# A graph layer on one core: the masks of four tiles by one compare, the degrees by folding

## What is computed

```python
mask = (adj > 0.0)                                   # (32, 256, 256)
diff = x[:, :, None, :] - x[:, None, :, :]
h    = relu((x @ W1[:F])[:, :, None, :] + diff @ W1[F:] + b1)
hm   = einsum('bjkh,bjk->bjh', h, mask)
deg  = sum(mask, axis=-1)
out  = layernorm(x + hm @ W2 + deg[..., None] * b2)
```

## Time and profile before

| | us |
|---|---|
| median of three runs | 307.55 |
| lowest, highest | 307.5, 307.82 |
| the profiled execution, its time | 308.28 |
| its span in the trace | 306.2 |
| PE, DVE, ACT, POOL busy | 278.8, 272.8, 239.5, 99.2 |
| masks (L1158), compares, 64 | 25.7 |
| masks (L1158), accumulator reads, 64 | 5.2 |

### The profile page before, as it was taken

One profiled execution on the slowest core, in us unless ns is written; L12 is line 12 of the kernel. 1 busy time (PEld: TensorE's weight loads), 2 busy tenths in 40 slices (PEclk: granted clock), 3 DMA queues, 4 the chain that ended last, 5 costly groups with the idle time before them and its releaser, 6 DMA issues. The chain is left out here.

```text
span 306.2 us, 9122 instructions
## 1 busy us (share of the span) xinstructions
PE 278.8 (91%) x2601; PEld 209.3 (68%) x2601; DVE 272.8 (89%) x987; ACT 239.5 (78%) x706; POOL 99.2 (32%) x166
## 2 busy tenths in 40 slices
PE   0496999999999999999999999999999999999960
PEld 0253676877777877868787777777786877776750
DVE  2886699999999999999999999999999999989761
ACT  2338788889898989899898989898979889876500
POOL 1306142313334342434232343433342323304111
PEclk9999899999999999999999999999999999999985
DMA  7920303030211303030402112030304020100000
GB/s 205 371 99 1 89 0 105 3 98 9 57 66 28 96 19 106 14 108 0 120 0 79 40 35 85 17 103 17 103 1 120 0 56 2 35 3 18 19 17 21
DMA packets 28833, 18.12 MB, mean 59 GB/s; under 512 B 17537, under 2 KB 28033, under 8 KB 28802
## 3 DMA queue, kind: packets, MB, share of 16 engines
q1 hardware_dynamic: 28802, 17.76, 19.7%
HBM read 15.65 MB, written 2.10 MB: 58 GB/s over the span
## 5 line engine op out<-in xcount | busy, mean ns | idle before, releaser
L1024 PE MATMUL ring<-hot,vh 128*128 128x256 bf16 (+3 forms) x448 | 96.7, 268 | 1.0 <-ACT ring L740 1.0
L1024 PE MATMUL ring<-hot,vl 128*128 128x256 bf16 (+3 forms) x448 | 96.2, 267 | 0.0
L740 ACT COPY ring<-um 128x512 f32<-128x512 f32 (+2 forms) x144 | 65.9, 474 | 19.5 <-DVE small L1302 10.8
L1293 DVE SCALAR_TENSOR_TENSOR sm<-ring,sm 128x512 f32<-128x512 f32 (+2 forms) x144 | 73.0, 507 | 7.0 <-PE ring L1024 3.3
L1293 DVE SCALAR_TENSOR_TENSOR st<-ring,st 128x256 f32<-128x256 f32 (+2 forms) x144 | 48.0, 334 | 5.5 <-PE ring L1030 2.1
L1024 PEld LDWEIGHTS ring<-hot,vh 128*128 128x128 f16 x448 | 43.9, 98 | 11.9 <-issue 7.3
L1269 DVE TENSOR_SCALAR hot<-slotT 128x1024 bf16<-128x1024 f16 (+2 forms) x144 | 49.2, 373 | 0.0
L740 ACT COPY ring<-ut 128x512 f32<-128x512 f32 (+7 forms) x128 | 38.5, 338 | 13.0 <-DVE st L1293 11.0
L1024 PEld LDWEIGHTS ring<-hot,vl 128*128 128x128 f16 x448 | 44.1, 98 | 2.6
L1030 PE MATMUL ring<-hot,vh 128*64 128x512 bf16 (+3 forms) x256 | 44.7, 353 | 0.0
L533 POOL TENSOR_TENSOR vl<-vf,vh 128x384 f16<-128x384 f32 x32 | 28.6, 914 | 47.0 <-ACT vh L702 47.0
(11 more groups left out here) (106 smaller groups left out, 560.6 us busy)
## 6 DMA issues: line engine op xcount, KB each, us to landing
adj_sb<-adj SPq DMA_DIRECT2D x16, 512.0 KB, 4.1
x_sb<-x SPq DMA_DIRECT2D x16, 128.0 KB, 2.2
x_all<-x SPq DMA_DIRECT2D x4, 512.0 KB, 7.9
xT_sb<-xT SPq DMA_DIRECT2D x16, 128.0 KB, 3.8
out<-o_sb SPq DMA_DIRECT2D x16, 128.0 KB, 2.0
wts<-weights SPq DMA_DIRECT2D x1, 513.0 KB, 4.8
cst_general<-general SPq DMA_DIRECT2D x1, 256.0 KB, 6.3
cst_half<-half SPq DMA_DIRECT2D x1, 113.5 KB, 3.5
```

Of the source, the lines that this page charges most:

```text
L740: eng.copy(view(segment, ring[unit % BANKS]), u).then_inc(seeded, 1)
L1024: last = eng.matmul(b[:, g * n:g * n + n], part[side][:, g * NT + k, 0:P], selection(g * NT + k), start=(s == 0 and not seeds), stop=(s == ...
L1293: eng.scalar_tensor_tensor(out=to, in0=v, scalar=0.0, in1=to, op0=ALU.max, op1=ALU.add).then_inc(added[tile], 1)
```

## The change

`mask_tile` goes. In its place stand five functions on DVE, each one instruction:

- `masks`: one compare over the 4 x 256 columns, without a sum;
- `halve`: bf16 addition of the two halves of every tile's row, 4 x 128 results;
- `quarter`: 4 x 64 results;
- `eighth`: 4 x 32 results;
- `degrees`: a sum over the last 32 of each tile (TENSOR_REDUCE), 4 results in fp32, which adds 4 to `degrees_ready`.

Per pair, eight DVE instructions become five. New semaphores (`masked`, `halved`, `quartered`, `eighthed`) order them among themselves. `masks` stands where tile 0 was, `halve` where tile 1 was, `quarter` and `eighth` where tile 2 was, `degrees` where tile 3 was. In the two places of the prologue all five stand in a row. The waits for the readers of `deg` move from the compare to `degrees`. No instruction of PE, ACT, POOL or SP is moved or changed.

```diff
@@ -282,6 +282,7 @@
 
         mask = both("mask", [P, TILES, N], BF16)
         deg = both("deg", [P, TILES])
+        halves, quarters, eighths = (sb(f"fold{n}", [P, TILES, n], BF16) for n in (N // 2, N // 4, N // 8))
         deg16 = both("deg16", [P, TILES], BF16)
         neg_key = sb("neg_key", [P, TILES])
         rank = sb("rank", [P, TILES])
@@ -343,6 +344,7 @@
         xT_loaded = [sem(f"xT_loaded{s}") for s in range(2)]
         stored = [sem(f"stored{s}") for s in range(2)]
         banks_set = sem("banks_set")
+        masked, halved, quartered, eighthed = sem("masked"), sem("halved"), sem("quartered"), sem("eighthed")
         degrees_ready = sem("degrees_ready")
         deg16_ready, neg_keys_ready = sem("deg16_ready"), sem("neg_keys_ready")
         keys_ready = sem("keys_ready")
@@ -1146,17 +1148,44 @@
             eng.memset(ones32[:, :], 1.0).then_inc(weights_ready, 1)
             eng.memset(ones[:, :], 1.0).then_inc(consts_ready, 1)
 
-            def mask_tile(pair, c):
-
-                if c == 0:
-                    eng.wait_ge(adj_loaded[pair.side], 16 * (pair.half + 1))
-                    if pair.follows(2):
-                        eng.wait_ge(maskT_ready, 2 * (pair.n - 1))
-                        eng.wait_ge(excess_ready, pair.n - 1)
-                        eng.wait_ge(neg_keys_ready, pair.n - 1)
-                        eng.wait_ge(db_ready, pair.n - 1)
-                eng.tensor_scalar(mask[pair.side][:, c, :], adj_sb[pair.side][:, c, :], 0.0, 0.0, ALU.is_gt,
-                                  ALU.add, accum_out=deg[pair.side][:, c:c + 1]).then_inc(degrees_ready, 1)
+            def masks(pair):
+
+                eng.wait_ge(adj_loaded[pair.side], 16 * (pair.half + 1))
+                if pair.follows(2):
+                    eng.wait_ge(maskT_ready, 2 * (pair.n - 1))
+                if pair.follows(1):
+                    eng.wait_ge(halved, pair.n)
+                eng.tensor_scalar(mask[pair.side][:, :, :], adj_sb[pair.side][:, :, :], 0.0, None,
+                                  ALU.is_gt).then_inc(masked, 1)
+
+            def halve(pair):
+                eng.wait_ge(masked, pair.n + 1)
+                if pair.follows(1):
+                    eng.wait_ge(quartered, pair.n)
+                eng.tensor_tensor(halves[:, :, :], mask[pair.side][:, :, 0:N // 2], mask[pair.side][:, :, N // 2:N],
+                                  ALU.add).then_inc(halved, 1)
+
+            def quarter(pair):
+                eng.wait_ge(halved, pair.n + 1)
+                if pair.follows(1):
+                    eng.wait_ge(eighthed, pair.n)
+                eng.tensor_tensor(quarters[:, :, :], halves[:, :, 0:N // 4], halves[:, :, N // 4:N // 2],
+                                  ALU.add).then_inc(quartered, 1)
+
+            def eighth(pair):
+                eng.wait_ge(quartered, pair.n + 1)
+                if pair.follows(1):
+                    eng.wait_ge(degrees_ready, TILES * pair.n)
+                eng.tensor_tensor(eighths[:, :, :], quarters[:, :, 0:N // 8], quarters[:, :, N // 8:N // 4],
+                                  ALU.add).then_inc(eighthed, 1)
+
+            def degrees(pair):
+                eng.wait_ge(eighthed, pair.n + 1)
+                if pair.follows(2):
+                    eng.wait_ge(deg16_ready, pair.n - 1)
+                    eng.wait_ge(neg_keys_ready, pair.n - 1)
+                    eng.wait_ge(db_ready, pair.n - 1)
+                eng.tensor_reduce(deg[pair.side][:, :], eighths[:, :, :], AX.X, ALU.add).then_inc(degrees_ready, TILES)
 
             def permutation(pair):
                 eng.wait_ge(ranks_ready, pair.n + 1)
@@ -1185,8 +1214,11 @@
                 eng.tensor_reduce(x_max1[:, :], x_max[:, :], AX.X, ALU.max).then_inc(scale_step, 1)
                 eng.wait_ge(w_sums_ready, 1)
                 eng.tensor_reduce(w_top[:, :], ring[0][:, 0:2 * H], AX.X, ALU.max).then_inc(scale_step, 1)
-                for c in range(TILES):
-                    mask_tile(next_one, c)
+                masks(next_one)
+                halve(next_one)
+                quarter(next_one)
+                eighth(next_one)
+                degrees(next_one)
                 eng.wait_ge(x_turned, 1)
                 eng.tensor_reduce(x_top[:, :], ring[1][0:1, 0:P], AX.X, ALU.max).then_inc(scale_step, 1)
                 eng.wait_ge(x_top_spread, 1)
@@ -1374,13 +1406,13 @@
                 if has(0):
                     selections(pair, 6, 7)
                 if has(2):
-                    mask_tile(second, 0)
+                    masks(second)
                 if has(-3):
                     moment(elder)
                 if has(-1):
                     add(old, 5)
                 if has(2):
-                    mask_tile(second, 1)
+                    halve(second)
                 if has(-1):
                     add(old, 6)
                 if has(0):
@@ -1410,13 +1442,14 @@
                     add(old, 10, 0, 1)
                     clamp_small(old, 10)
                 if has(2):
-                    mask_tile(second, 2)
+                    quarter(second)
+                    eighth(second)
                 if has(-2):
                     add_residual(older)
                 if has(0):
                     selections(pair, 9, NHOT)
                 if has(2):
-                    mask_tile(second, 3)
+                    degrees(second)
                 if has(-1):
                     reduce_small(old)
                 if has(0):
@@ -1427,8 +1460,11 @@
                 if has(0):
                     add(pair, 1)
 
-            for c in range(TILES):
-                mask_tile(Pair(0, 0), c)
+            masks(Pair(0, 0))
+            halve(Pair(0, 0))
+            quarter(Pair(0, 0))
+            eighth(Pair(0, 0))
+            degrees(Pair(0, 0))
             eng.wait_ge(consts_loaded["half"], 16)
             eng.tensor_copy(ident[:, :], const("ident16")).then_inc(consts_ready, 1)
             absolute_weights()
...
```

More of the change, by code:

```diff
@@ L1444, in general @@
                 side = pair.side
-                for c in range(TILES):
-                    mask_tile(pair, c)
+                masks(pair)
+                halve(pair)
+                quarter(pair)
+                eighth(pair)
+                degrees(pair)
                 permutation(pair)
```

## The result

| | us |
|---|---|
| before, median (lowest, highest) | 307.69 (307.5, 308.0) |
| after, median (lowest, highest) | 311.7 (310.65, 312.5) |
| ratio, 95% interval | 1.0125 (1.0092 to 1.0158) |
| after, profiled execution, its span | 312.38, 310.6 |

The change costs about 4 us. The forecast was 311.9, within 308.5 to 316. That the total agrees does not mean that every step does: the steady bodies lost less than was forecast, and other things made up for it. The ratios leave out executions more than 1.5% above the fastest of their kernel, which are two of the ten of `pad_384` and none elsewhere.

The account below looks back on a forecast made before the run. PE was taken to bound the kernel, with DVE level behind it. Bodies 3 to 13 (3.4 us), body 1 (0.28) and the prologue (0.61) made 4.3 on a median of 307.55: 311.9 us, range 308.5 to 316.

Parts of the forecast that it names:

- Prices of the five instructions: On DVE, masks 0.695, halve 0.416, quarter 0.279, eighth 0.211, degrees 0.276 us; in a body 1.59 against 1.34.
- One wait: On DVE, eighth waits for quarter just ahead, so its start comes 0.04 us after quarter's end.
- The masks: In DVE's bodies, the wide compare adds 0.275 us ahead of start_tail and start_main.
- Rivals 1 and 2: PE keeps pace (wide compare 0.42), 307.9 to 308.2, chance 0.12 with in-between cases; or wide compare 1.21, 318.6, chance 0.08.
- `halve` and `centre`: In bodies from the fourth on, POOL's centre holds DVE's halve, adding 0.11 us a body.
- The prologue and body 1: Pair 1's chain of five ahead of x_top adds 0.61 us; masks in body 1 add 0.28.
- DVE has 0.05 to spare, and time added beyond that is paid in full: In steady bodies, DVE has 0.05 us of slack on average; any DVE time beyond it lengthens the body.
- Bodies 12 and 13: Last two of the eleven bodies 3 to 13, each forecast to lose 0.31 us, 3.4 in all.
- DVE is full: In bodies 3 to 13 DVE is full, so 0.25 + 0.11 - 0.05 = 0.31 us is lost in each.
- Rival 3: More locks with POOL in the bodies, on masks too or halve by the full 0.47: up to 315.9 us, chance 0.10.
- Rival 4: Instruction count decides, not overlap: DVE gains 0.09 us a body, PE's waits shrink, 306.4 to 307.0, chance 0.05.

Follow-up runs that it names:

- pad_384: Kernel before plus one DVE max over 384 fp32 columns behind tile 0 in every mask-making body: 309.83 us, ratio 1.0031 to before.
- pad_64: Kernel before plus one DVE max over 64 fp32 columns behind tile 0 in every mask-making body: 307.91 us, ratio 0.9996 to before.
- after_light: Kernel after with layer norm statistics done for one tile of four, 0.39 us less DVE a body: 310.82 us, ratio 1.0101 to before.
- after_xl: Kernel after with POOL's second x subtraction (xl) moved behind centre, nothing else: 309.63 us, ratio 1.0034 to before.

## Why the prediction was right, and where it was not

- **Prices of the five instructions: right.** 0.683 (0.695 forecast), 0.42 unheld (0.416), 0.28 (0.279), 0.23 (0.211), 0.280 (0.276). The means of `quarter` and `eighth` above are higher only through body 0, where POOL works beside them; the prediction has POOL idle at the later foldings. DVE's timeline there:

```profile
30.27 1.02 DVE L1172 TENSOR_TENSOR fold<-fold 128x256 bf16<-128x256 bf16 x1
31.32 0.77 DVE L1179 TENSOR_TENSOR fold<-fold 128x128 bf16<-128x128 bf16 x1
```

  One wait was priced too low. In the bodies 4 to 11, those of the hardware loop, `eighth` starts 0.13 us behind the end of `quarter`, not 0.04 (0.03 to 0.04 in the others), which makes the five 1.68 us a body there instead of 1.59, locks left out. It lies outside the stretch that counts. DVE's timeline:

```profile
132.52 0.28 DVE L1172 TENSOR_TENSOR fold<-fold 128x256 bf16<-128x256 bf16 x1
132.93 0.23 DVE L1179 TENSOR_TENSOR fold<-fold 128x128 bf16<-128x128 bf16 x1
```

  The masks cost 0.26 us more than a tile where they stand (from their start to the next instruction, 141.24 to 141.84, 0.60 against 0.33 or 0.34), 0.275 forecast. Rivals 1 and 2 fall with the first of them.
- **`halve` and `centre`: right in kind.** 0.53 to 0.61 us instead of 0.42, ending 0.2 to 0.3 after `centre`; +0.11 was forecast, and the `add` behind it starts 0.12 or 0.20 later.
- **The prologue and body 1: together about right.** `x_top` comes 0.69 us later instead of 0.61, in two kernels. But up to the third `turn_perm` only 0.72 is left of that and of the 0.28 of body 1, where 0.89 were forecast. That the profiled runs differ there by twice as much is the landing of the weights.
- **"DVE has 0.05 to spare, and time added beyond that is paid in full": the step that failed.** The two bodies that I compared at `start_tail` are DVE's late and early ones, and the wait of 0.09 in the early one ends at PE's `project`; how long the `add` ahead could have been late I didn't work out. `pad_64` puts the spare at 0.1 or more, and the trace of `pad_384` at 0.21 where xl holds the selection. With 0.26 for the masks and 0.12 or 0.20 for the lock, less 0.21, and 0.02 or 0.08 by which xl lets the masks start later (10.95 or 11.01 instead of 10.93), a body grows by 0.19 or 0.33: the 16.87 and 17.01 that the steady bodies show in turn.
- **Bodies 12 and 13 were counted like the rest.** Before, they already took 16.97 and 16.84 us, and DVE stood idle in the first of them. Its timeline in before:

```profile
223.62 0.55 DVE L1293 SCALAR_TENSOR_TENSOR sm<-ring,sm 128x384 f32<-128x384 f32 x1
224.45 0.87 DVE L1246 SCALAR_TENSOR_TENSOR st<-ut,bx 64x256 f32<-64x256 f32 x2 [0.28 <-issue]
```

  They lose 0.19 together, not 0.62. With 9 x 0.284 = 2.55 for the others this is the 2.74; the term was 0.7 too large. The profiled executions agree with the forecast all the same (312.38; 308.28 and the 4.3 of the sum give 312.6), because the weights landed 0.7 us later: 308.28 + 1.43 + 2.74 = 312.45. That is luck. The medians, of four executions each, are known to 1 us and can't tell the 4.3 of the forecast from the 3.5 that the traces have without the weights.
- **"DVE is full": right for the sum, wrong as the cause.** The number of the period came out near because the masks and the lock stand in the loop through xl as well, and because two errors, the spare (0.05 for 0.21) and the lock (0.11 for up to 0.20), partly cancel. A remedy drawn from it, less work anywhere on DVE, can be worth nothing in the steady bodies (`after_light`), and one that it would not have named, POOL's order, is worth 2.2 us. The row that could have told is a group of DVE in before:

```profile
L1269 DVE TENSOR_SCALAR hot<-slotT 128x384 bf16<-128x384 f16 x16 | 6.0, 375 | 0.0
```

  Half as much again as the 0.25 of one that isn't held. I had looked for locks only on instructions that the change makes.
- **Rival 3** (more locks) named `masks` and a longer `halve`. `halve` was longer, by half of what the rival had at most, and `masks` was held once in one experiment. The lock that mattered was on a neighbour.
- **Rival 4** (the count of instructions) is out: eight instructions became five and DVE's busy time rose by 4.8 us. The accumulator read that the change saves was hidden anyway. By the Trainium skill (VectorE: DVE Perf Modes, Rules for kernel authors) it is the count of operations that should be kept small, not the semaphores; this case differs. Here an instruction that isn't waited for overlaps its neighbour by 0.08 us, and a semaphore between two neighbours takes that away and adds 0.03 to 0.13.
- **The page on the shared port** (the Trainium skill, SBUF — State Buffer, Who interferes with whom) agrees with every lock seen: the 16-bit selections, `halve` and the small sums are held beside POOL's two-input work, the tile compare with its accumulator never is (0.40 to 0.42 us in all 64). That makes the old form worth more than its length in a place where POOL is active.

## What to carry to other kernels

When an engine shows no idle time, that says nothing on whether its work or its locks fill it: compare the mean of each group with its shortest member, and follow a stretched one to what ran beside it, before believing that less work helps. A saving is worth testing with an instruction taken out elsewhere: if the period doesn't move, that stretch of the engine's order isn't on the bound, which may be a loop that passes through another stretch of it. Cutting the number of instructions pays only where each is waited for; a chain of small dependent ones in place of independent ones can cost more than it saves.

## Not expected of the hardware

- The lock works both ways. `halve` is held by `centre`, 0.53 to 0.62 us instead of 0.42 with xl near it or not; in `after_xl`, xl starts while `halve` still runs, and takes 0.85 instead of 0.67.
- In the kernel before, the selection of 928 columns lost the race against POOL's `db` in up to every second body (mean 0.606 us); in the kernel after, with a period longer by 0.28, it won nearly always (0.466). That is 0.14 us of DVE a body given back by chance, in a kernel that couldn't use it. `after_xl` can, and part of its 16.70 may rest on it; that wasn't taken apart.
- The same additions cost more on POOL than on DVE: the first one, 128x512, took 1.15 us there against 0.42 unheld, the second 0.67 against 0.28.
